# Causal mask of a softmax attention half: eight constant rows in the query and key stacks, and small triangles in place of whole mask tiles

## The reference

```
q = (x @ Wq + bq);  k = (x @ Wk + bk);  v = (x @ Wv + bv)          # 16 heads of 16
scores = einsum('bthd,bshd->bhts', q, k) / sqrt(16)
scores = scores + alibi                  # alibi = -slope[h] * abs(t - s), T = 1024 (the inner B, S, D are not used)
scores = where(s > t, -inf, scores)      # causal
out = einsum('bhts,bshd->bthd', softmax(scores), v) @ Wo + bo
```

## Time and profile before

| | |
|---|---|
| median of 3 runs | 2726.83 us (2723.98 to 2726.88) |
| profiled execution | 2732.81 us, span of its instructions 2730.7 us |
| mean granted clock of TensorE | 0.923 |
| busy | PE 83%, DVE 62%, ACT 46%, POOL 29% |
| second pass: first stack load to the end | 1125 to 2731 us |

### The profile page before, as it was taken

The page is one execution under the profiler, slowest core; times in us unless marked ns, Lnnn a source line. Parts: engine busy times, 40 slices in busy tenths (PEclk is TensorE's granted clock), DMA queues, the critical chain, the costliest instruction groups (busy, mean ns, idle before and its releaser), DMA issues.

```text
span 2730.7 us, 57194 instructions
## 1 busy us (share of the span) xinstructions
PE 2267.1 (83%) x24094; PEld 1196.8 (44%) x24195; DVE 1702.9 (62%) x3805; ACT 1261.3 (46%) x2025; POOL 783.0 (29%) x658
## 2 busy tenths in 40 slices
PE   3568887988889766488899999999999989998964
PEld 1346555665556543223244443443444434433332
DVE  5647566565654544367677676776777767667327
ACT  2323434343342212135565655666656655655623
POOL 2224232323311111523143243351533513202110
PEclk9789999999999978679899999999999999999977
DMA  2101010010100111321122122230321201202053
GB/s 83 47 17 48 32 48 32 32 48 19 45 17 32 48 47 47 106 79 59 64 93 87 48 85 66 68 111 24 102 78 63 80 30 64 70 26 96 27 216 123
DMA packets 127439, 171.33 MB, mean 63 GB/s; under 512 B 8864, under 2 KB 94880, under 8 KB 127184
## 3 DMA queue, kind: packets, MB, share of 16 engines
q1 hardware_dynamic: 123088, 167.15, 18.3%
q10 hardware_dynamic: 4096, 0.53, 0.1%
HBM read 91.11 MB, written 76.02 MB: 61 GB/s over the span
## 4 chain that ended last, share of the span: by engine, by line
PE 64%; DVE 17%; ACT 7%; issue 4%; DMA 3%; ACTq 3%; SPq 2%; POOL 1%; DVEq 0%; POOLq 0%
PE general L885 10%; PE general L562 9%; PE out_of_heads L763 9%; PE scores L704 6%; PE scores L680 4%; PE general L896 4%; PE general L548 4%; DVE maxima L1399 3%; PE turned_scores L718 3%; ACTq L1104 3%; PE general L528 3%; PE out_of_heads L636 2%; DMA k_stacks<-k_stack 2%; PE out_of_heads L646 2%; PE scores L594 2%
## 5 line engine op out<-in xcount | busy, mean ns | idle before, releaser
L1399 DVE TENSOR_REDUCE maxima<-scores 128x1 f32<-128x512 f32 (+3 forms) x1536 | 798.0, 553 | 392.5 <-PE scores L680 241.7
L1083 ACT ACTIVATE probs_turned<-turned_scores 128x512 f32<-128x512 f32 x1152 | 682.8, 600 | 531.5 <-PE turned_scores L680 282.8
L704 PE MATMUL scores<-k_stacks,q_stacks 51*128 51x512 bf16 (+3 forms) x1536 | 455.0, 341 | 74.5 <-DVE maxima L1399 47.9
L718 PE MATMUL turned_scores<-q_stacks,k_stacks 53*128 53x512 bf16 (+3 forms) x1536 | 446.2, 334 | 39.7 <-ACT probs_turned L1083 39.6
L704 PEld LDWEIGHTS scores<-k_stacks,q_stacks 51*128 51x128 bf16 x1536 | 125.7, 95 | 325.3 <-DVE maxima L1399 196.1
L680 PE MATMUL scores<-mask_scores,identity 64*128 64x256 bf16 (+3 forms) x954 | 250.8, 263 | 0.0
L680 PE MATMUL turned_scores<-mask_turned,identity 64*128 64x128 bf16 (+3 forms) x969 | 249.8, 258 | 0.0
L1704 POOL TENSOR_TENSOR ln_low<-ln 128x512 bf16<-128x512 f32 x128 | 138.5, 1089 | 283.1 <-DVE ln L1381 283.1
L1683 POOL TENSOR_SCALAR ln<-x_for_attention,ln_mean_var,ln_rstd 128x256 f32<-128x256 f32 x104 | 128.2, 1243 | 209.1 <-DVEq L1478 119.3
L1621 POOL TENSOR_TENSOR state_low<-state_doubled,state_high 128x2048 bf16<-128x2048 f32 x14 | 57.0, 4072 | 380.6 <-ACT state_high L1016 380.6
L680 PEld LDWEIGHTS scores<-mask_scores,identity 64*128 64x128 bf16 (+1 forms) x954 | 90.5, 95 | 165.9 <-issue 85.5
(11 more groups left out here) (231 smaller groups left out, 5171.5 us busy)
## 6 DMA issues: line engine op xcount, KB each, us to landing
x_after_attention<-x_residual SPq DMA_DIRECT2D x16, 1024.0 KB, 5.2
x_times_wo<-x_wo_out SPq DMA_DIRECT2D x64, 256.0 KB, 2.2
k_stacks<-k_stack SPq DMA_DIRECT2D x64, 212.0 KB
q_stacks<-q_stack SPq DMA_DIRECT2D x64, 204.0 KB
x_for_attention<-in_x SPq DMA_DIRECT2D x8, 1024.0 KB, 5.3
x_residual<-in_x SPq DMA_DIRECT2D x8, 1024.0 KB, 5.3
x_for_attention<-x_after_attention SPq DMA_DIRECT2D x8, 1024.0 KB, 12.1
ffn_h<-x_times_wo SPq DMA_DIRECT2D x32, 256.0 KB, 6.9
```

The source lines that it names most:

```text
L704: mx = pe.matmul(bank_s[:, first * P:(first + tiles) * P], QS[at:at + QROWS, r, i * P:(i + 1) * P], KS[at:at + QROWS, r, k0 * P:(k0 + tile ...
L718: ex = pe.matmul(bank_t[:, first * P:(first + tiles) * P], KS[at:at + KROWS, r, j * P:(j + 1) * P], QS[at:at + KROWS, r, i0 * P:(i0 + tile ...
L1083: nc.scalar.activation(PR[:, s % SLOTS, :], TB[s % 2][:, :], ACT.Exp).then_inc(sem["ex_taken"], 1)
L1399: r = dve.tensor_reduce(MP[:, gg % 2, g, at:at + 1], max_bank[m][:, first * P:(first + tiles) * P], AX.X, ALU.max)
```

## The change

Eight rows are added to both stacks (`MASK_ROWS` to `QROWS`), so `QROWS` becomes 59 and `KROWS` 61. Row r of the eight is non-zero only in tile r: in the query stack 1 in the first 64 columns of tile r, in the key stack `NEG` in its second 64 columns. Their product adds `NEG` to the quarter of each diagonal tile where the first 64 queries meet the second 64 keys, within the product that is made anyway. What remains of a diagonal tile are two triangles of 64x64. `triangles` adds them with two products a piece (n = 0, 1), each of 64 contraction rows in the row tile of the piece itself, with 64 moving columns for one diagonal tile and 128 for two. A second identity, with its halves exchanged (`ident_x`), serves the triangle that lies in the other 64 output rows. The two halves of the mask in different row tiles, the filling pair between them and the wait for `half_masked` are gone.

The constants come from VectorE (`set_mask_rows`, in the first pass after `set_state`: a memset of 128x2048, a reduce, a copy and a multiply of 128x512) and four transfers on SP (two a stack buffer), which SP issues once in the first pass.

```diff
-QROWS = ROWS + 3
-KROWS = ROWS + 5
+MASK_ROWS = ROWS + 3
+QROWS = MASK_ROWS + NT
+KROWS = QROWS + 2
...
+        HM = flat(OL[:, :, :]).rearrange("p (s t) -> p s t", s=2)
...
+                    sp.wait_ge(sem["mask_rows"], 1)
+                    for par in range(2):
+                        for n, dram in enumerate((q_dram, k_dram)):
+                            sp.dma_start(dram[par, :, MASK_ROWS:QROWS, :], HM[:, n, :]).then_inc(sem["mask_stored"], 16)
...
+            def triangles(bank, pieces, mask, at_end, at, n):
+
                 blocks = [first + tiles - 1 if at_end else first
                           for i, k0, tiles, first in pieces if (k0 + tiles == i + 1 if at_end else i == k0)]
...
+                rows_ = slice(at, at + HALF_ROWS)
+                eye = (ident, ident_x)[(n + at // HALF_ROWS) % 2][rows_, :]
+                columns = bank[:, :].rearrange("p (a b) -> p a b", b=HALF_ROWS)
+                first, last = 2 * blocks[0] + n, 2 * blocks[-1] + n
+                step = max(last - first, 1)
+                m = mask[rows_, rows_].rearrange("p (a b) -> p a b", a=1).broadcast_to(
+                    [HALF_ROWS, len(blocks), HALF_ROWS])
+                return pe.matmul(columns[:, first:last + 1:step, :], eye, m, start=False, stop=(n == 1))
...
-                halves = [slice(HALF_ROWS * n, HALF_ROWS * (n + 1)) for n in range(2)]
-                if (mask_max or mask_ex) and len(post) and 0 <= s < STEPS:
-                    own_row, other = s % 2, 1 - s % 2
+                for n in range(2):
                     if mask_max:
-                        masked(bank_s, MAX_UNITS[u], mask_s, True, halves[other], False).then_inc(sem["half_masked"], 1)
+                        mx = triangles(bank_s, MAX_UNITS[u], mask_s, True, at_s, n)
                     if mask_ex:
-                        masked(bank_t, EXP_UNITS[ue], mask_t, False, halves[own_row], False
-                               ).then_inc(sem["half_masked"], 1)
-                    fill_slot(s, b, k, post[0])
-                    post = post[1:]
-                    pe.wait_ge(sem["half_masked"], w.next("half_masked", int(mask_max) + int(mask_ex)))
...
-                else:
-                    if mask_max:
-                        mx = masked(bank_s, MAX_UNITS[u], mask_s, True)
-                    if mask_ex:
-                        ex = masked(bank_t, EXP_UNITS[ue], mask_t, False)
+                        ex = triangles(bank_t, EXP_UNITS[ue], mask_t, False, at_t, n)
...
+            def set_mask_rows():
+
+                dve.memset(HM, 0.0)
+                step(dve.tensor_reduce(tile_of_row[:, :], ident32[:, :].rearrange("p (h t) -> p t h", t=NT),
+                                       AX.X, ALU.add))
+                own_tile = tile_of_row[:, :].rearrange("p (t a) -> p t a", a=1).broadcast_to([P, NT, HALF_ROWS])
+                at = [HM[:, n, :].rearrange("p (t a b) -> p t a b", a=2, b=HALF_ROWS)[:, :, n, :] for n in range(2)]
+                dve.tensor_copy(at[0], own_tile)
+                dve.tensor_scalar(at[1], own_tile, NEG, None, ALU.mult).then_inc(sem["mask_rows"], 1)
...
+                    set_mask_rows()
```

More of the change, by code:

```diff
@@ L148, in mixer_kernel @@
             "pk_low", "pk_sent0", "pk_sent1", "pk_sent2", "pk_sent3", "pk_in0", "pk_in1", "pk_in2",
-            "half_done", "half_masked", "mx_full", "mx_taken", "mx_ready", "mx_parts", "mx_turned", "mx_row", "mx_sent0", "mx_sent1",
+            "half_done", "mx_full", "mx_taken", "mx_ready", "mx_parts", "mx_turned", "mx_row", "mx_sent0", "mx_sent1",
             "ex_full", "ex_taken", "probs_used", "ot_ready", "ot_turned",
@@ L201, in mixer_kernel @@
         ident = sb("identity", [P, P], BF16)
+        ident_x = sb("identity_halves_swapped", [P, P], BF16)
         ident32 = sb("identity_fp32", [P, P], F32)
+        tile_of_row = sb("tile_of_mask_row", [P, NT], F32)
         mask_t = sb("mask_turned", [P, P], BF16)
@@ L450, in _ @@
             sp.wait_ge(sem["w_split"], 8)
+            sp.wait_ge(sem["mask_stored"], 64)
             for b in range(-2, B + 1):
@@ L693, in attend @@
                     gg, u, g = m // GROUP, m % GROUP // HEADS, (m % HEADS) ^ 1
-                    r, at = 2 * (gg % 3) + g // 2, SLOT * (g % 2)
+                    r, at_s = 2 * (gg % 3) + g // 2, SLOT * (g % 2)
                     if m % GROUP == 0:
@@ L704, in attend @@
                         mx = pe.matmul(bank_s[:, first * P:(first + tiles) * P],
-                                       QS[at:at + QROWS, r, i * P:(i + 1) * P],
-                                       KS[at:at + QROWS, r, k0 * P:(k0 + tiles) * P],
+                                       QS[at_s:at_s + QROWS, r, i * P:(i + 1) * P],
+                                       KS[at_s:at_s + QROWS, r, k0 * P:(k0 + tiles) * P],
                                        start=(n == 0), stop=not mask_max)
@@ L709, in attend @@
                     gg, ue, g = s // GROUP, s % GROUP // HEADS, s % HEADS
-                    r, at = 2 * (gg % 3) + g // 2, SLOT * (g % 2)
+                    r, at_t = 2 * (gg % 3) + g // 2, SLOT * (g % 2)
                     if s % GROUP == 0:
@@ L718, in attend @@
                         ex = pe.matmul(bank_t[:, first * P:(first + tiles) * P],
[L719 to L720 removed]
+                                       KS[at_t:at_t + KROWS, r, j * P:(j + 1) * P],
+                                       QS[at_t:at_t + KROWS, r, i0 * P:(i0 + tiles) * P],
                                        start=(n == 0), stop=not mask_ex)
[L722 to L724 removed]
+                for n in range(2):
                     if mask_max:
[L726 removed]
+                        mx = triangles(bank_s, MAX_UNITS[u], mask_s, True, at_s, n)
                     if mask_ex:
[L728 to L741 removed]
+                        ex = triangles(bank_t, EXP_UNITS[ue], mask_t, False, at_t, n)
                 if mx is not None:
@@ L1298, in _ @@
             dve.tensor_copy(ident32[:, :], stage[:, 0:P])
+            for n in range(2):
+                dve.tensor_copy(ident_x[:, HALF_ROWS * n:HALF_ROWS * (n + 1)],
+                                stage[:, HALF_ROWS * (1 - n):HALF_ROWS * (2 - n)])
             dve.tensor_copy(own[:, :], stage[:, 4 * P:4 * P + SW])
@@ L1643, in chunks_low @@
             def chunks_low(bb, half):
+                if bb == 0 and half == 0:
+                    pool.wait_ge(sem["mask_stored"], 64)
                 pool.wait_ge(sem["o_taken1"], NT * bb + NT // 2 * (half + 1))
```

12 lines of the change are left out of this document (2 added, 10 removed).

## The result

| | time, us (median, range) | span of the profiled execution, us | mean granted clock |
|---|---|---|---|
| before | 2726.86 (2723.98 to 2737.09) | 2730.7 | 0.923 |
| after | 3145.52 (3142.61 to 3149.48) | 3147.4 (execution 3149.48) | 0.858 |

The changed kernel is slower: the ratio is 1.1522, with a 95% interval of 1.1501 to 1.1544. The forecast of 3145 us and its mechanism held.

What follows compares the result with a forecast made beforehand. Bound: each interval is 24 TensorE steps or the stack load on one DMA engine, whichever is longer, plus 12 steps. Span 2730.7 + 40 + 382 - 3 = 3150 us, so median about 3145 us; range 3045 to 3260.

Steps and rivals of the forecast that it cites:

- The load: The four stack transfers feeding TensorE: 480 packets on one DMA engine at 80 ns each, 40.8 us from issue to landing.
- The interval: Time between first uses of successive stack loads: load plus 12 further steps, 57.4 us instead of 44.24, 29 times, +382 us.
- The stall: TensorE waiting for k_stacks before each first use: about 14 us in each of 29 groups, some 400 us in all.
- The 24 steps: TensorE's steps that run while the next load is under way: 28.6 us before, 26.6 us after the change.
- The mask products: TensorE's masked steps: 0.96 to 0.98 us with filling, 0.21 us less without; at most 113 us of TensorE.
- Setting the constants: set_mask_rows on VectorE ahead of the first masking, 3.3 us, plus 0.1 for the second identity: +3.4 us, between 0 and 5.
- The start: First loads through one engine: third group's first use at 1263 us instead of 1223.13, +40 us, between 30 and 50.
- After the last use: The last 48 steps, with no load ahead of them, get shorter by the mask saving: -3 us.
- A: Rival, faster: the load keeps its spread and grows by bytes only, or uses more engines; 2690 or 2665 us; chance 0.08.
- B: Rival, slower still: stores and input loads queue on the crowded engine, 5 us more an interval, 3290 us; chance 0.08.
- C: Rival: load as slow as forecast, but the 12 steps after it take 12 us; 52.8 an interval, 3010 us; chance 0.05.
- D: Rival, no change: a load of about 30 us that eats exactly the gain; chance 0.01.

Runs made afterwards that it cites:

- the kernels with 48 and with 47 rows: Changed kernel, each stack transfer cut after 48 rows: 2645.41 us; kernel before, each q_stacks transfer of 51 rows cut into 47 and 4: 2971.27 us.
- the kernel with the old products: Changed kernel's rows, loads and constant rows, with the mask products of the kernel before in place of the triangles: 3167.09 us, ratio 1.1600.
- all loads cut: Each stack transfer cut in two, the first 48 rows and the rest: changed kernel 2645.41 us, kernel before 2700.88 us.

## Why the prediction was right, point by point

- **The load.** 40.8 us by 480 packets of 80 ns on one engine; the 29 loads took 40.50 to 42.00 us from issue to use, 40.9 in the mean. Up to 1.4 us come in one group of four, the one in which SP issues `x_residual<-x_after_ffn` right behind the load. The step on which all rests, that 59 and 61 behave as 53 does, is shown by the closing packets, the share of one sixteenth, and the kernels with 48 and with 47 rows. No view names the engine: that all four transfers use the same one is inferred from the 480 packets that follow each other at 80 ns.
- **The interval.** 57.4 forecast, 57.51 measured. Its part after the use was put at 15.0 - 0.9 + 2.5 = 16.6 and took 16.56 in the mean (14.6 to 19.8). The single terms are less exact than their sum. The mask's share is nearer 0.5 us than 0.9, by the kernel with the old products. The clock's is nearly as forecast: over the first 15 us after each use the granted clock is 0.795 in the mean, which is the low level for 6.2 of them, about 3.1 us lost. In the kernel before it was 0.945 over the same stretch, 0.8 us lost, which the 15.0 already hold; so 2.3 us were added, for 2.5 forecast. The part itself was 15.1 us before. 15.1 - 0.5 + 2.3 makes 16.9, some 0.3 more than measured, and this rest is open. In the group shown the stall ran at 0.56 and the first product of 512 columns took 0.60 us, where it takes 0.39 at full clock.
- **The stall.** 14 us in 29 groups, some 400 in all; measured 379.6 us in these 29, 13.1 each. The 24 steps were put at 26.6 us and take 27.8 (40.9 - 13.1). They start from 29.1 us in the mean before, where the forecast took the 28.6 of one group, and with all loads cut they shrink from 29.1 to 27.7, by 1.4 us and not 2.0. This term has no part in the sum, as the load covers it.
- **The mask products.** Of the two kinds of step, both sizes held. A masked step with filling (PE timeline), against the earlier trace rows:

```profile
1841.65 0.32 PE L714 MATMUL scores<-k_stacks,q_stacks 59*128 59x384 bf16 x1
...
1842.65 0.32 PE L714 MATMUL scores<-k_stacks,q_stacks 59*128 59x384 bf16 x1
```

1.00 us here, and 0.96 in the other row tile of the same step (1841.67 to 1842.63), for 0.96 to 0.98 forecast and 1.14 before. One without filling, against the earlier trace rows:

```profile
1903.58 0.22 PE L728 MATMUL turned_scores<-q_stacks,k_stacks 61*128 61x128 bf16 x1
...
1903.84 1.48 PE L758 MATMUL out_of_heads<-probs_turned,values 128*17 128x512 f32 x8
```

0.26 us, as forecast, for 0.47. Over all steps with three pairs of filling products, four mask products and the full clock, after 1300 us, the mean falls from 1.11 to 0.96 us. The upper bound of 113 us of TensorE was 101 in busy time with the loads cut. Of it 55 us reach the end when no load is in the way, and in the changed kernel about 22 (3167.09 less 3145.52). No cost of the weight loads of the 64-column triangles shows: both kinds of step last what their columns give.
- **Setting the constants.** The chain in order of time, against the earlier trace rows:

```profile
92.08 0.91 DVE attention_out_low L1334
92.99 0.17 DVE tile_of_mask_row L1335
93.17 0.02 issue
93.19 0.43 DVE attention_out_low L1339
93.62 0.34 DVE attention_out_low L1340
93.95 1.19 DVE probs_turned L1354 x2
```

2.0 us stand ahead of the masking, where 3.3 were forecast. The term at fault is the memset: 0.91 us, not the 1.78 of the fp32 row I had taken as its like. The trace has these 2048 bf16 columns as 1024 of uint32, half as many elements as that row. The copies took 0.43 and 0.34 for 0.6 each. SP issues the four transfers from 93.98 us on in 2.5 us, and POOL's waits hold none for them.
- **The start.** +40 forecast, +37.2 measured; the second load's use is at 1217.53 us for 1221.4 forecast. The +3.4 for the constants did not come through: the first load is issued at 1124.98 us, where it was 1125.10 before. In the pair with all loads cut it is 1.3 us later (1123.00 and 1121.70), so the delay exists and is lost in other waits here. The two loads' 32.0 us took 31.5 (1217.53 against 1186.00), and the rest lies within the bounds.
- **After the last use.** -3 forecast, -5.1 measured.
- **The sum.** The start came out 2.8 us under its term, the intervals 2.6 over (384.6 for 382) and the end 2.1 under, so the span is 3147.4 us for 3150. The profiled execution then stood 4.0 us above the median of its runs, where the forecast took over the 6.0 of the kernel before. This noise made up for the rest: the last 2 us of the agreement are luck.
- **The rivals.** A (the load by its bytes) fails on the closing packets and on the 40.6 us. B (queueing that adds 5 us to each interval) is there at a quarter of its size, in one group of four. C fails on the 12 steps, which took 16.6 us and not 12. D (a load of some 30 us) fails on the 40.6 us too.

## What to carry over

Before lengthening a DMA, write down its slowest dimension and how that number divides: here 51 to 59 rows and 53 to 61, 15% more bytes, cost 15% of the kernel (that the two are equal is chance, as bytes cost nothing here), and cutting off 48 of them turned the loss into a gain of 3.1% over the kernel before. A small DMA share of the page says nothing when it is one engine of sixteen that works all the time: look for a share near 0.06 and a rate that stays flat through a transfer. Work taken off an engine that then waits is worth nothing, and even with no load in the way only about half of what came off TensorE reached the end, the rest standing in its waits for VectorE and ScalarE.

## What the runs showed of the hardware that was not expected

A crowded engine holds up the queue that feeds it. With 59 and 61 rows SP needs 0.24, 2.94, 9.51 and 9.48 us to issue the four transfers of one load, 22.3 us in all, against 3.2 us for the eight spread ones. What stands behind them in SP's queue waits too: in a neighbouring group the next transfer, a store from another tensor, is stuck for another 10 us (SP timeline):

```profile
1800.24 10.94 SPq L391 DMA_DIRECT2D k_stacks<-k_stack  x1
1811.22 10.10 SPq L313 DMA_DIRECT2D q_stack<-qk_high  x1
```

GpSimd feels it: its waits for `ffn_h<-x_times_wo`, which SP issues behind these stores, are 135.8 us in all, where they were 29.1 before and 23.6 with all loads cut. They are not on the path that ended last, on which `k_stacks` hold 27 of DMA's 28%. The hold-up of the queue is also where the 15% of SP's queue in the chain come from. Those 15% are the same wait as that for the DMA, seen from the issuing side, and not a second one: the engine moves the load at one flat rate from start to end, whenever SP gets to issue the next transfer.
